# A gated delta-rule layer on one core: four prologues hoisted in front of one stream of 64 heads, sixteen heads written out in the loop's body

## The chip, the core and the metric

The kernel runs on one core of one Trainium2 chip. The metric is device time in microseconds (us). The engines are TensorE (PE, with its weight loads PEld), VectorE (DVE), ScalarE (ACT), GpSimd (POOL) and SyncE (SP), whose queue issues every DMA of this kernel.

## What is computed

Eight sequences of 512 tokens and 256 channels pass through a gated delta-rule attention layer (16 key heads, each with a group of 2 value heads of 128 channels) and a feed-forward block with ternary weights. Cut to what matters here:

```
qkvz = layernorm(x) @ W_qkvz          # per key head: q, k, v, z
qkv  = silu(causal_conv1d(qkv))       # 4 taps
g, beta = decay and gate from layernorm(x) @ W_ba
per chunk of 64 tokens:
    attn = (I + tril(k_beta k^T * decay))^-1
    v'   = attn @ v_beta - k_cumdecay @ state
    out  = q @ state * exp(g) + tril(q k^T * decay) @ v'
    state = state * exp(g_last) + (k * decay)^T @ v'
out = rmsnorm(out * silu(z)) @ W_out  # summed over the heads
```

The feed-forward block works on the same normalized tokens; its result plus `x` is what the heads' outputs are added to (`acc`).

## The kernel before, in words

The batch is cut into four groups of two sequences (`NQ` = 4, `TOK` = 1024 tokens). The four groups are the turns of an outer loop, which every engine runs for itself. A turn has these stages:

- **Prologue.** `x` is loaded into `acc`, normalized and transposed into `xnT` (the transposed tokens that all projections read), the decays and gates are computed, and the feed-forward block is added into `acc`. SP reloads the prepared feed-forward weights and the scan mask (L417 to L419) in each turn, and at the end writes the rows and columns that the heads read (`g_rows`, `ge_rows`, `gel_d`, `cols_d`) to memory and waits for them.
- **Heads.** A head has two halves. Its *front* (`front_piece`, 24 places) projects q, k, v, z, convolves, builds the decay matrix `at` and inverts its triangular part; `at` goes out to memory and comes back in another layout (`relayout`, whose first DMA is `a_d<-at`, L383, one in each head). Its *core* runs over the 8 chunks in order, and its output is projected and added to `acc` up to three chunks later.
- `weave` runs the core of one head with the front of the next head threaded through it, three places of the front at each chunk. `head_passes` (L276) puts a turn together: the front of head 0 by itself, a weave, a loop of 7 iterations with two weaves written out in its body, the core of head 15 by itself, and `last_tile` for the chunks still owed.
- **Store.** When the last `accumulate` is done, SP writes `acc` to `out`, waits until it has landed, and the next turn begins.

The engines meet twice in a turn (`meet`, L270: each drains, adds to a semaphore and waits for all five), before the prologue and behind it. Between the meetings the order of work is that of the code on each engine, held together by counting semaphores, whose targets are worked out in registers from the head's number `g` (L239, L243, L247). `load_weights` (L338) fetches the projection weights `wt` of a head once the last projection of the head before is done, `load_rest` its decay rows `gb`, `qge`, `gel` and its output weights `wo`.

Of the kernel before, what the change touches and what calls it, by code (L numbers as in the profile page):

```python
# [13 lines left out]
P = 128  # L14
# [41 lines left out]
def build(nc, x_in, w_qkvz, w_ba, conv_w, a_log, dt_bias, norm_w, w_out, w_gu, w_proj, consts, out):  # L56
    ctx = ExitStack()
    with ctx:
# [10 lines left out]
        g_rows = dram("g_rows", [HK, NB, NC, GRP, CH])  # L69
        ge_rows = dram("ge_rows", [HV, NC, NB, CH])  # L70
        gel_d = dram("gel_d", [HV, NB, NC])
        cols_d = dram("cols_d", [HK, P, COLS * U])
        a_d = dram("a_d", [P, U, CH])
        x_d = dram("x_d", [P, 2, BLK, BLK])
        wgu_d = dram("wgu_d", [P, KD * 2 * FFN], BF16)
        wp_d = dram("wp_d", [P, FFN // P * D])
# [15 lines left out]
        acc = sb("acc", [P, TILES, D])  # L92
        wt = sb("wt", [P, KD, HEADCOLS])
# [100 lines left out]
        d_const, d_wraw, d_wsave = sem("d_const"), sem("d_wraw"), sem("d_wsave")  # L194
# [123 lines left out]
        def _(sp):  # L318
# [32 lines left out]
            def load_rest(g, p, hk):  # L351
# [5 lines left out]
                             cols_d[bass.ds(hk, 1), :, :].rearrange("a p x -> p (a x)")).then_inc(d_g, 16)  # L357
                for b in range(NB):
                    row = g_rows[bass.ds(hk, 1), b, :, :, :].rearrange("k c h t -> k (c h t)")
# [4 lines left out]
                row = ge_rows.rearrange("(k h) c b t -> k (h c b t)", h=GRP)[bass.ds(hk, 1), :]  # L364
# [5 lines left out]
                             gel_d.rearrange("(k h) b c -> k (h b c)", h=GRP)[bass.ds(hk, 1), :].to_broadcast(  # L370
# [4 lines left out]
                    :, bass.ds(hk * GRP, GRP), :]).then_inc(d_wo, 16)  # L375

# [34 lines left out]

            with sp.Fori(0, NQ) as q:
                meet(sp, 2 * q + 1)
# [11 lines left out]
                for b in range(NB):  # L425
                    rows = slice(b * HV, (b + 1) * HV)
                    for h in range(GRP):
                        sp.dma_start(g_rows[:, b, :, h, :], g_t[b * HV + h:(b + 1) * HV:GRP, :].rearrange(
                            "k (c t) -> k c t", t=CH)).then_inc(d_rows, 16)
                    sp.dma_start(ge_rows[:, :, b, :], ge_t[rows, :].rearrange("p (c t) -> p c t", t=CH)).then_inc(d_rows, 16)  # L430
                    sp.dma_start(gel_d[:, b, :], gelc[rows, :]).then_inc(d_rows, 16)
                sp.wait_ge(colev, (q + 1) * (2 * COLS))
                apart(sp)
                sp.dma_start(cols_d.rearrange("k p x -> p k x"),
                             colstage.rearrange("p k s u -> p k (s u)")).then_inc(d_rows, 16)
                sp.wait_ge(d_rows, (q + 1) * (16 * (NB * (GRP + 2) + 1)))
# [3 lines left out]
                sp.wait_ge(d_wq, (q + 1) * 48)  # L440
                apart(sp)
                meet(sp, 2 * q + 2)

                load_rest(q * HK, 0, 0)
                relayout(q * HK)
                relayout_back(q * HK)
                with sp.Fori(0, HK // 2 - 1) as j:
                    for n in range(2):
                        g, hk = q * HK + j * 2 + (n + 1), j * 2 + (n + 1)
                        load_weights(g, hk)  # L450
                        load_rest(g, (n + 1) % 2, hk)
                        relayout(g)
                        relayout_back(g)
                load_weights(q * HK + (HK - 1), HK - 1)
                load_rest(q * HK + (HK - 1), 1, HK - 1)
                relayout(q * HK + (HK - 1))
                relayout_back(q * HK + (HK - 1))

                before(sp, "accs", q * HK + HK)
                apart(sp)  # L460
                for b in range(NB):
                    sp.dma_start(out.rearrange("b s d -> (b s) d")[bass.ds(q * TOK + b * SEQ, SEQ), :].rearrange(
                        "(c t) d -> t c d", t=CH), acc[half(b), :, :]).then_inc(d_out, 16)
                sp.wait_ge(d_out, (q + 1) * (16 * NB))
                apart(sp)


        @block.tensor
        def _(pe):
# [16 lines left out]
            def prologue(q):  # L486
# [18 lines left out]
                pe.wait_ge(d_wq, (q + 1) * 48)  # L505
# [222 lines left out]
            def front_piece(g, p, s):  # L728
# [7 lines left out]
                for n, at_s in enumerate((1, 2, 4, 5, 5, 8, 10, 13, 13, 14, 14, 16, 17, 20, 22, 22, 23, 23)):  # L736
                    if s == at_s:
                        fill_ring(g, p, n)
# [24 lines left out]
            def front(g, p):  # L763
                for s in range(3 * NC):
                    front_piece(g, p, s)

            def core(g, p, fill=lambda s: None, first=False):
# [3 lines left out]
            def last_tile(g, p):  # L771
# [5 lines left out]
            def weave(g, p, first=False):  # L777
                core(g, p, lambda s: front_piece(g + 1, 1 - p, s), first)

            with pe.Fori(0, NQ) as q:  # L780
                meet(pe, 2 * q + 1)
                prologue(q)
                meet(pe, 2 * q + 2)
                head_passes(pe, q, front, core, weave, last_tile)
# [3 lines left out]
        def _(act):  # L788
# [148 lines left out]
            def front_piece(g, p, s):  # L937
# [21 lines left out]
            def core(g, p, fill=lambda s: None, first=False):  # L959
# [13 lines left out]
            def last_tile(g, p):  # L973
# [5 lines left out]
            def front(g, p):  # L979
                for s in range(3 * NC):  # L980
                    front_piece(g, p, s)

            def weave(g, p, first=False):
                core(g, p, lambda s: front_piece(g + 1, 1 - p, s), first)

            with act.Fori(0, NQ) as q:
                meet(act, 2 * q + 1)
                prologue(q)
                meet(act, 2 * q + 2)
                head_passes(act, q, front, core, weave, last_tile)  # L990
# [3 lines left out]
        def _(dve):  # L994
# [41 lines left out]
            def prologue(q):  # L1036
# [41 lines left out]
                def decay_step(n):  # L1078
# [16 lines left out]
                    if n == 4:  # L1095

                        dve.wait_ge(d_wq, (q + 1) * 48)
# [71 lines left out]
            def decayed_squares(g, p, x):  # L1169
                if x == 0:  # L1170
                    before(dve, "yp", g)
                    loaded(dve, d_off, g - 1, NB * (NBLK - 1))
# [104 lines left out]
            def front_piece(g, p, s):  # L1277
# [28 lines left out]
            def core(g, p, fill=lambda s: None, first=False):  # L1306
                for c in range(NC):
# [5 lines left out]
                    if three:  # L1313
                        accumulate(*three)
# [7 lines left out]
            def last_tile(g, p):  # L1322
                mean_square(g, p, NC - 1)
                for j in (NC - 3, NC - 2, NC - 1):
                    accumulate(g, p, j)

            def front(g, p):
                for s in range(3 * NC):
                    front_piece(g, p, s)

            def weave(g, p, first=False):
                core(g, p, lambda s: front_piece(g + 1, 1 - p, s), first)

            with dve.Fori(0, NQ) as q:
                meet(dve, 2 * q + 1)
                prologue(q)
                meet(dve, 2 * q + 2)
                head_passes(dve, q, front, core, weave, last_tile)
# [3 lines left out]
        def _(pool):  # L1342
# [33 lines left out]
            def front_piece(g, p, s):  # L1376
# [5 lines left out]
            def core(g, p, fill=lambda s: None, first=False):  # L1382
# [10 lines left out]
            def last_tile(g, p):  # L1393
                rms(g, p, NC - 1)

            def front(g, p):
                for s in range(3 * NC):
                    front_piece(g, p, s)

            def weave(g, p, first=False):  # L1400
                core(g, p, lambda s: front_piece(g + 1, 1 - p, s), first)

            with pool.Fori(0, NQ) as q:
                meet(pool, 2 * q + 1)
                prologue(q)
                meet(pool, 2 * q + 2)
                head_passes(pool, q, front, core, weave, last_tile)
# [18 lines left out]
```

## Time and profile before

| | |
|---|---|
| runs shown | 5644.02, 5653.62, 5666.7 us (median 5653.62) |
| profiled execution, its own time | 5670.83 us |
| its span, first to last instruction | 5668.7 us |
| mean granted TensorE clock | 0.948 |
| PE busy | 4973.4 us, 88% of the span |
| DVE, ACT, POOL busy | 62%, 54%, 19% |
| one turn (from one load of `x` to the next) | 1397.6, 1392.5 and 1394.6 us |

The profiled execution's own time is 2.1 us over its span and 0.3% over the median of the runs. The shares are of the span; PE counts as busy while a matmul runs, and its weight loads are a column of their own.

### The profile page before, as it was taken

The numbers are of one execution on the slowest core, as the hardware profiler recorded it, in microseconds if no ns is written. First come the engines' busy times: TensorE is split into PE (matmuls) and PEld (weight loads), VectorE is DVE, ScalarE is ACT, GpSimd is POOL, SyncE is SP. The second block draws the span as 40 slices with busy tenths as digits, with TensorE's granted clock in tenths as the row PEclk, the third lists the DMA queues.
The fourth block names the chain that finished last, engine by engine and source line by source line (L and its number), as shares of the span: only waits on it lengthen the run. The fifth ranks groups of instructions, "written<-read, shape, count | busy, mean of one in ns | idle before, by whom it ended". The sixth has DMA issues, their size and how long they took to land.

```text
span 5668.7 us, 144560 instructions
## 1 busy us (share of the span) xinstructions
PE 4973.4 (88%) x52244; PEld 3458.8 (61%) x52272; DVE 3513.1 (62%) x6423; ACT 3046.6 (54%) x7910; POOL 1063.6 (19%) x1064
## 2 busy tenths in 40 slices
PE   3899999999779999999977999999997899999898
PEld 1566666666556666666645666666664566666666
DVE  6466666666446666666645666666664666666665
ACT  2355555555346555555524655555552555555555
POOL 0022221222111212221211221222220122221122
PEclk7899999999989999999988999999998999999999
DMA  2121222222122221222112222212211221222221
GB/s 68 48 57 42 58 56 53 59 48 53 39 53 54 58 59 43 56 57 54 42 38 59 56 58 53 59 42 58 57 34 44 70 56 46 56 57 54 53 49 38
DMA packets 685930, 296.71 MB, mean 52 GB/s; under 512 B 598976, under 2 KB 642112, under 8 KB 675648
## 3 DMA queue, kind: packets, MB, share of 16 engines
q1 hardware_dynamic: 685120, 286.09, 21.0%
q8 instruction: 486, 7.96, 0.6%
q14 instruction: 324, 2.65, 0.1%
HBM read 213.55 MB, written 59.78 MB: 48 GB/s over the span
## 4 chain that ended last, share of the span: by engine, by line
PE 62%; DVE 11%; ACT 9%; issue 8%; SPq 5%; DMA 3%; DVEq 0%; POOL 0%; ACTq 0%; POOLq 0%
PE pj L587 10%; PE dsb L724 8%; PE ms L645 7%; SPq L409 5%; PE pj L582 4%; ACT arena L856 4%; PE pot L682 4%; PE pot L653 4%; DVE cy L1135 4%; PE dsb L696 3%; PE pod L665 3%; PE ms L600 3%; PE pod L708 2%; PE ms L614 2%; PE pj L577 2%
## 5 line engine op out<-in xcount | busy, mean ns | idle before, releaser
L587 PE MATMUL pj<-xnT,wt 128*128 128x512 f32 x2048 | 1037.2, 636 | 101.0 <-ACT arena L856 58.7
L1135 DVE SCALAR_TENSOR_TENSOR cy<-xpad,cw,cy 128x1024 f32<-128x1024 f32 x768 | 1059.7, 1386 | 33.3 <-ACT cy L876 23.7
L1374 POOL TENSOR_TENSOR rout<-rin,expo 128x2 f32<-128x2 f32 x512 | 366.8, 716 | 2738.7 <-DVE rin L1270 2738.7
L724 PE MATMUL dsb<-wo,yT 128*128 128x256 f32 x2048 | 609.6, 423 | 98.5 <-issue 94.3
L587 PEld LDWEIGHTS pj<-xnT,wt 128*128 128x128 f32 x2048 | 369.1, 198 | 528.4 <-issue 372.7
L1368 POOL TENSOR_TENSOR sdec<-st,gel 128x512 f32<-128x512 f32 x384 | 402.2, 1047 | 1047.5 <-DVE st L1259 866.2
L875 ACT ACTIVATE xpad<-pj 128x512 f32<-128x512 f32 x512 | 302.5, 591 | 500.5 <-PE pj L587 499.7
L934 ACT ACTIVATE yT<-dsb 128x256 f32<-128x256 f32 x512 | 196.2, 383 | 644.6 <-PE dsb L715 643.2
L582 PE MATMUL pj<-wt,xnT 128*128 128x256 f32 x2048 | 511.7, 393 | 0.0
L724 PEld LDWEIGHTS dsb<-wo,yT 128*128 128x128 f32 x2048 | 365.9, 199 | 217.7 <-issue 180.5
L1249 DVE SCALAR_TENSOR_TENSOR rr<-pot,nge,arena 128x128 f32<-128x128 f32 x896 | 271.2, 344 | 338.6 <-PE pot L653 338.6
L582 PEld LDWEIGHTS pj<-wt,xnT 128*128 128x128 f32 x2048 | 371.4, 191 | 86.5 <-issue 43.9
L1259 DVE TENSOR_TENSOR st<-dsb,sdec 128x512 f32<-128x512 f32 x384 | 264.8, 690 | 220.9 <-PE dsb L696 216.5
L929 ACT ACTIVATE arena<-arena,rout 128x128 f32<-128x128 f32 x1024 | 351.6, 393 | 43.4 <-POOL rout L1374 43.0
L923 ACT ACTIVATE junk<-arena 128x128 f32<-128x128 f32 x1024 | 306.4, 307 | 96.0 <-issue 53.7
L1270 DVE SCALAR_TENSOR_TENSOR rin<-ss,qe 128x2 f32<-128x2 f32 x512 | 80.1, 156 | 437.4 <-ACT junk L923 437.4
L876 ACT ACTIVATE cy<-pj,cw 128x512 f32<-128x512 f32 x512 | 348.4, 680 | 0.0
L696 PEld LDWEIGHTS dsb<-ww,arena 64*128 64x128 f32 x3584 | 238.4, 186 | 175.1 <-issue 167.0
L1275 DVE TENSOR_TENSOR acc<-dsb,acc 128x256 f32<-128x256 f32 x512 | 215.9, 422 | 201.0 <-PE dsb L724 192.9
L682 PE MATMUL pot<-rr,bda 64*64 64x128 f32 x3584 | 293.2, 281 | 53.7 <-DVE rr L1249 53.7
L696 PE MATMUL dsb<-ww,arena 64*128 64x128 f32 x3584 | 325.0, 297 | 16.5 <-ACT ww L917 16.4
L708 PE MATMUL pod<-ww,arena 64*64 64x128 f32 x4096 | 332.2, 281 | 2.3 <-ACT ww L917 2.3
(163 smaller groups left out, 8502.6 us busy)
## 6 DMA issues: line engine op xcount, KB each, us to landing
qge<-ge_rows SPq DMA_DIRECT2D x64, 1024.0 KB, 7.0
wt<-in_L_attn_W_qkvz SPq DMA_DIRECT2D x64, 768.0 KB, 4.4
gb<-g_rows SPq DMA_DIRECT2D x128, 256.0 KB, 4.1
a_d<-at SPq DMA_DIRECT2D x64, 512.0 KB, 2.6
wo<-in_L_attn_W_out SPq DMA_DIRECT2D x64, 256.0 KB, 2.7
x_d<-xpair SPq DMA_DIRECT2D x128, 128.0 KB, 1.7
ap_<-a_d SPq DMA_DIRECT2D x512, 16.0 KB, 1.8
dd<-x_d SPq DMA_DIRECT2D x512, 16.0 KB, 1.8
```

The source lines that it names most:

```text
L582: last = mm(pj[n % 2][:, v * GRP * DH:(v + 1) * GRP * DH], xnT[:, k, c * P:(c + 1) * P], wt[:, k, 4 * DH:4 * DH + GRP * DH], start=(k == 0 ...
L587: last = mm(pj[n % 2][:, :], wt[:, k, col:col + DH], batch(xnT, k, i), start=(k == 0), stop=(k == KD - 1))
L645: last = mm(ms[n][half(b), v * CH:(v + 1) * CH], pbd[half(b), u, :], src[half(b), u, :], start=True, stop=True, tile_position=(b * CH, b * ...
L682: last = mm(pkw[half(b), (GRP + h) * DH:(GRP + h + 1) * DH], bda[half(b), p, c * GRP + h, :], rhs, start=True, stop=True, tile_position=(b ...
L696: last = mm(dsb[:, b, h * DH:(h + 1) * DH], kkd[p][half(b), c * GRP + h, :], ww[half(b), h, :], start=True, stop=True, tile_position=(b * ...
L708: last = mm(po[half(b), h * DH:(h + 1) * DH], it[half(b), p, c * GRP + h, :], ww[half(b), h, :], start=(c == 0), stop=True, skip_group_che ...
L724: last = mm(dsb[:, 0, GRP * DH:GRP * DH + D], yT[:, h, :], wo[:, p, h, :], start=(h == 0), stop=(h == GRP - 1))
L876: last = fn(cy[:, m % 2, i, :], src[:, :], ACT.Copy, scale=cw[:, m, TAPS - 1:TAPS])
L929: last = fn(zz[p][:, j, h, :], zz[p][:, j, h, :], ACT.Copy, scale=rout[:, h:h + 1])
L1135: stt(y, x[:, :, tap:tap + SEQ], cw[:, kind, tap:tap + 1], y, ALU.mult, ALU.add).then_inc(S["conv"], 1)
L1368: tt(sdec[:, :, :, :], st[:, c % 2, :, :, :], bc(gel[:, p, :, :].rearrange("p h (b c) -> p b h c", b=NB)[:, :, :, c], 3, DH), ALU.mult).th ...
L1374: tt(rout[:, :], rin[:, :], expo[:, 0, 0:GRP], ALU.pow).then_inc(S["routs"], 1)
```

## The change

All engines now run the four prologues in one loop, and then the 64 heads as one stream (`head_stream`): the front of head 0, a weave, a loop of 3 iterations with sixteen weaves written out, 14 more weaves written out behind it, and the core of the last head. What a prologue leaves for its heads goes to memory with a place for each group: the rows and columns as before, and in addition `xnT_d` (1 MB, the transposed tokens) and `base_d` (1 MB, `x` plus the feed-forward block). When the stream comes to the first head of a group, SP loads that group's `xnT` behind `wt`, and `base` behind `wo`; the first head's `accumulate` reads `base` instead of `acc`. The output is stored in two parts while the next group's first heads run (chunks 0 to 4, then 5 to 7). The feed-forward weights stay on chip through the four prologues, so their saving and reloading is gone, and the scan mask is loaded once. In the body of the loop the head's number within its group is a constant, and in the stretches outside the loop all wait targets are.

```diff
-        def head_passes(eng, q, front, core, weave, last_tile):
-            front(q * HK, 0)
-            weave(q * HK, 0, True)
-            with eng.Fori(0, HK // 2 - 1) as j:
-                weave(q * HK + j * 2 + 1, 1)
-                weave(q * HK + j * 2 + 2, 0)
-            core(q * HK + (HK - 1), 1)
-            last_tile(q * HK + (HK - 1), 1)
+        def head_stream(eng, front, core, weave, last_tile):
+            front(0, 0)
+            weave(0, 0, True)
+            with eng.Fori(0, NQ - 1) as q:
+                for n in range(1, HK + 1):
+                    weave(q * HK + n, n % HK)
+            for n in range((NQ - 1) * HK + 1, NQ * HK - 1):
+                weave(n, n % HK)
+            core(NQ * HK - 1, HK - 1)
+            last_tile(NQ * HK - 1, HK - 1)
...
             sp.wait_ge(q_ev, 12)
-            sp.dma_start(wgu_d, wguT.rearrange("p k n -> p (k n)")).then_inc(d_wsave, 16)
-            sp.dma_start(wp_d, wpT.rearrange("p i n -> p (i n)")).then_inc(d_wsave, 16)
-            sp.wait_ge(d_wsave, 32)
+            sp.dma_start(scanmask, consts[:, SCANMASK:CONSTS]).then_inc(d_wq, 16)
+            sp.wait_ge(d_wq, 16)
...
+            def load_tokens(g, q):
+                sp.dma_start(xnT[:, :, :].rearrange("p k t -> p (k t)"), xnT_d[bass.ds(q, 1), :, :].rearrange(
+                    "q p x -> p (q x)")).then_inc(d_xn, 16)
...
+                if hk == 0:
+                    sp.dma_start(base[:, :, :].rearrange("p t d -> p (t d)"), base_d[bass.ds(q, 1), :, :].rearrange(
+                        "q p x -> p (q x)")).then_inc(d_base, 16)
...
+            def head(g, q, hk, weights=True, stores=True):
+                if weights:
+                    load_weights(g, hk)
+                if hk == 0:
+                    load_tokens(g, q)
+                load_rest(g, q, hk)
+                if hk == 1 and stores:
+                    store(q - 1, NC - 3, NC)
+                relayout(g)
+                relayout_back(g)
+                if hk == 0 and stores:
+                    after(sp, "accs", g - 1, NC - 3)
+                    apart(sp)
+                    store(q - 1, 0, NC - 3)
+
+            load_weights(0, 0)
+            meet(sp, 1)
             with sp.Fori(0, NQ) as q:
-                meet(sp, 2 * q + 1)
...
-                sp.dma_start(wguT.rearrange("p k n -> p (k n)"), wgu_d).then_inc(d_wq, 16)
-                sp.dma_start(wpT.rearrange("p i n -> p (i n)"), wp_d).then_inc(d_wq, 16)
-                sp.dma_start(scanmask, consts[:, SCANMASK:CONSTS]).then_inc(d_wq, 16)
-                load_weights(q * HK, 0)
+                sp.wait_ge(xntev, (q + 1) * (TILES // 2))
+                apart(sp)
+                sp.dma_start(xnT_d[bass.ds(q, 1), :, :].rearrange("q p x -> p (q x)"),
+                             xnT[:, :, :].rearrange("p k t -> p (k t)")).then_inc(d_rows, 16)
...
+                sp.wait_ge(facc, (q + 1) * TILES)
+                apart(sp)
+                sp.dma_start(base_d[bass.ds(q, 1), :, :].rearrange("q p x -> p (q x)"),
+                             acc[:, :, :].rearrange("p t d -> p (t d)")).then_inc(d_rows, 16)
...
-                meet(sp, 2 * q + 2)
...
+                meet(sp, q + 2)
+
+            head(0, 0, 0, weights=False, stores=False)
+            head(1, 0, 1, stores=False)
+            with sp.Fori(0, NQ - 1) as q:
+                for n in range(2, HK + 2):
+                    head(q * HK + n, q + n // HK, n % HK)
+            for n in range((NQ - 1) * HK + 2, NQ * HK):
+                head(n, NQ - 1, n % HK)
...
-            def fill_ring(g, p, n):
+            def fill_ring(g, p, n, new_tokens):
                 kind, i = ring[n]
                 if n == 0:
                     loaded(pe, d_w, g, 4)
+                    if new_tokens:
+                        pe.wait_ge(d_xn, g + HK)
...
-            def accumulate(g, p, j):
+            def accumulate(g, hk, j):
+                if hk == 0 and j == 0:
+                    dve.wait_ge(d_base, g + HK)
+                if hk == 0 and j in (0, NC - 3) and not (type(g) is int and g == 0):
+                    dve.wait_ge(d_out, g * 4 + (0 if j else -32))
                 after(dve, "od", g, j + 1)
-                tt(acc[:, j, :], dsb[:, 0, GRP * DH:GRP * DH + D], acc[:, j, :], ALU.add).then_inc(S["accs"], 1)
+                tt(acc[:, j, :], dsb[:, 0, GRP * DH:GRP * DH + D], (acc if hk else base)[:, j, :], ALU.add
+                   ).then_inc(S["accs"], 1)
```

On PE, in the program before, this is what stands at the end of the loop's body: the last chunk of the second weave, and the branch back to its first (`L577` is the last turned `v`, `L280` the loop).

```order
L645 MATMUL ms<-at,pbd 64x64 x16
L239 REGISTER_ALU
L708 MATMUL pod<-ww,arena 64x128 x4
L239 REGISTER_ALU
L577 MATMUL pj<-cst,vT 128x128 x4
L239 REGISTER_ALU
L577 MATMUL pj<-cst,vT 128x128 x4
L280 REGISTER_ALU
L280 COMPARE_AND_BRANCH
```

In the changed program the same last chunk, at the end of the second weave of the written-out body, runs into the first projection of the output in the third weave (`L754` is what was L724, `L607` what was L577).

```order
L675 MATMUL ms<-at,pbd 64x64 x16
L241 REGISTER_ALU
L738 MATMUL pod<-ww,arena 64x128 x4
L241 REGISTER_ALU
L607 MATMUL pj<-cst,vT 128x128 x4
L241 REGISTER_ALU
L607 MATMUL pj<-cst,vT 128x128 x4
L754 MATMUL dsb<-wo,yT 128x256 x2
L745 MATMUL dsb<-cst,arena 128x128 x2
L241 REGISTER_ALU x2
```

The register step and the branch are gone from this place; they stand once, behind the sixteenth weave. Behind the loop, in the weaves whose numbers are constants, PE's code has no register rows at all; this is its start:

```order
L283 COMPARE_AND_BRANCH
L754 MATMUL dsb<-wo,yT 128x256 x2
L745 MATMUL dsb<-cst,arena 128x128 x2
L712 MATMUL pot<-arena,bda 64x128 x4
L617 MATMUL pj<-xnT,wt 128x512 x2
L726 MATMUL dsb<-ww,arena 128x128 x4
```

On SP's queue, in the program before, a group ends with the return of the last head's inverse, the store of `out`, and the branch of the outer loop.

```order
L409 DMA ee<-x_d 16x16x16 x8
L243 ISA
L462 DMA out<-acc 64x8x256 x2
L412 REGISTER_ALU
L412 COMPARE_AND_BRANCH
```

In the changed program the queue goes from a group's first head (its inverse returns, `L427`) over the first part of the store (`L361`) to the weights of the second head (`L347`).

```order
L427 DMA ee<-x_d 16x16x16 x8
L241 REGISTER_ALU
L361 ISA
L361 DMA out<-acc 64x5x256
L361 ISA
L361 DMA out<-acc 64x5x256
L241 REGISTER_ALU
L245 ISA
L347 DMA wt<-in_L_attn_W_qkvz 128x2x768
```

The store, with its wait for five accumulations of the head before, now stands ahead of a load of weights, where it stood alone.

## Rows read from the trace of the kernel before

**Rows 1.** The page: span; PE's busy time and instructions; a queue that carries instructions.

```profile
span 5668.7 us, 144560 instructions
PE 4973.4 (88%) x52244; PEld 3458.8 (61%) x52272; DVE 3513.1 (62%) x6423; ACT 3046.6 (54%) x7910; POOL 1063.6 (19%) x1064
...
q8 instruction: 486, 7.96, 0.6%
```

**Rows 2.** Busy time by stage: prologue, weaves, core alone; then clock, DMA share, GB/s.

```profile
94.00:207.00 113.00, 87.88 (x441) 56.18 (x448) 54.53 (x103) 31.90 (x54) 8.30 (x9) 0.88 0.15 45
...
365.00:1420.00 1055.00, 967.25 (x10640) 676.77 (x10639) 688.12 (x1270) 611.59 (x1626) 218.92 (x218) 0.97 0.23 54
1420.00:1487.00 67.00, 51.00 (x604) 38.52 (x600) 28.08 (x66) 26.89 (x95) 13.32 (x17) 0.97 0.08 18
```

**Rows 3.** SP's queue in order of time: start, duration, line; setup and first two turns.

```profile
86.91 0.35 SPq L334 DMA_DIRECT2D wgu_d<-arena  x1
...
93.82 1.60 SPq L415 DMA_DIRECT2D acc<-in_L_attn_x  x2
...
207.41 0.36 SPq L356 DMA_DIRECT2D cols<-cols_d  x1
...
231.65 0.33 SPq L383 DMA_DIRECT2D a_d<-at  x1
...
1491.41 1.56 SPq L415 DMA_DIRECT2D acc<-in_L_attn_x  x2
...
1603.07 0.36 SPq L356 DMA_DIRECT2D cols<-cols_d  x1
...
1626.12 0.33 SPq L383 DMA_DIRECT2D a_d<-at  x1
```

**Rows 4.** SP's queue: `a_d<-at` of heads 1, 3, 4, 5, 15 of group 0.

```profile
297.48 0.33 SPq L383 DMA_DIRECT2D a_d<-at  x1
...
447.78 0.33 SPq L383 DMA_DIRECT2D a_d<-at  x1
...
528.23 0.33 SPq L383 DMA_DIRECT2D a_d<-at  x1
...
602.39 0.33 SPq L383 DMA_DIRECT2D a_d<-at  x1
...
1387.37 0.33 SPq L383 DMA_DIRECT2D a_d<-at  x1
```

**Rows 5.** The same, last head of a group and first of the next, twice.

```profile
2780.03 0.33 SPq L383 DMA_DIRECT2D a_d<-at  x1
...
3020.25 0.32 SPq L383 DMA_DIRECT2D a_d<-at  x1
...
4173.00 0.34 SPq L383 DMA_DIRECT2D a_d<-at  x1
...
4415.01 0.32 SPq L383 DMA_DIRECT2D a_d<-at  x1
```

**Rows 6.** Waits: who, what ended them, us in total, times, longest.

```profile
PE dsb L724 <- issue: 94.3, 24, 4.9
...
POOL gb L1356 <- DMA gb<-g_rows: 255.9, 8, 45.8
```

**Rows 7.** The chain that ended last: start, us, what; a loop's branch, then the outer loop's.

```profile
495.27 3.95 issue
...
1488.23 2.72 issue
```

**Rows 8.** Busy time by engine right behind that first branch, granted clock third from the end.

```profile
499.30:503.00 3.70, 3.70 (x15) 2.55 (x16) 1.24 (x3) 0.84 (x4) 2.57 (x2) 0.54 0.02 7
```

**Rows 9.** DMA issues: count, KB each, median us from issue to landing.

```profile
arena<-wgu_d SPq DMA_DIRECT2D x4, 1024.0 KB, 8.5
...
cols_d<-arena SPq DMA_DIRECT2D x4, 512.0 KB, 3.9
```

**Rows 10.** Register steps of L247 on the weight loads' sequencer: ns shortest/median/longest.

```profile
L247 PEldq FUSED_REGOPS  x192: 37/37/51, 207.0 to 5596.3; - x192
```

More of the change, by code:

```diff
@@ L66, in dram @@
             return nc.dram_tensor(name, shape, dt, kind="Internal").ap()
[L69 to L72, printed above, removed]
+        g_rows = dram("g_rows", [NQ, HK, NB, NC, GRP, CH])
+        ge_rows = dram("ge_rows", [NQ, HV, NC, NB, CH])
+        gel_d = dram("gel_d", [NQ, HV, NB, NC])
+        cols_d = dram("cols_d", [NQ, HK, P, COLS * U])
+        xnT_d = dram("xnT_d", [NQ, P, KD * TOK])
+        base_d = dram("base_d", [NQ, P, TILES * D])
         a_d = dram("a_d", [P, U, CH])
         x_d = dram("x_d", [P, 2, BLK, BLK])
-        wgu_d = dram("wgu_d", [P, KD * 2 * FFN], BF16)
-        wp_d = dram("wp_d", [P, FFN // P * D])
         cst = sb("cst", [P, SCANMASK])
@@ L92, in build @@
         acc = sb("acc", [P, TILES, D])
+        base = sb("base", [P, TILES, D])
         wt = sb("wt", [P, KD, HEADCOLS])
@@ L349, in load_weights, with store, load_rest @@
                     "(h p) t -> p h t", h=GRP)).then_inc(d_w, 16)
-            def load_rest(g, p, hk):
+            def load_tokens(g, q):
+                sp.dma_start(xnT[:, :, :].rearrange("p k t -> p (k t)"), xnT_d[bass.ds(q, 1), :, :].rearrange(
+                    "q p x -> p (q x)")).then_inc(d_xn, 16)
+            def store(q, j0, j1):
+                for b in range(NB):
+                    sp.dma_start(out.rearrange("b s d -> (b s) d")[
+                        bass.ds(q * TOK + (b * SEQ + j0 * CH), (j1 - j0) * CH), :].rearrange("(c t) d -> t c d", t=CH),
+                        acc[half(b), j0:j1, :]).then_inc(d_out, 16)
+            def load_rest(g, q, hk):
+                p = hk % 2
                 before(sp, "coef", g)
@@ L439, in _ @@
                 apart(sp)
-                sp.wait_ge(d_wq, (q + 1) * 48)
-                apart(sp)
-                meet(sp, 2 * q + 2)
[L444 to L465, printed above, removed]
+                meet(sp, q + 2)
[6 more added lines that the diff above has]
+                head(n, NQ - 1, n % HK)
+            for j0, j1 in ((0, NC - 3), (NC - 3, NC)):
+                after(sp, "accs", NQ * HK - 1, j1)
+                apart(sp)
+                store(NQ - 1, j0, j1)
+            sp.wait_ge(d_out, NQ * (4 * 16))
         @block.tensor
@@ L761, in core_step, with front, core, last_tile @@
                 fill(3 * c + 2)
-            def front(g, p):
+            def front(g, hk):
                 for s in range(3 * NC):
-                    front_piece(g, p, s)
-            def core(g, p, fill=lambda s: None, first=False):
+                    front_piece(g, hk, s)
+            def core(g, hk, fill=lambda s: None, first=False):
+                p = hk % 2
                 for c in range(NC):
                     core_step(g, p, c, fill, first)
-            def last_tile(g, p):
+            def last_tile(g, hk):
+                p = hk % 2
                 out_project(g, p, NC - 3)
@@ L775, in last_tile, with weave @@
                     out_project(g, p, j)
-            def weave(g, p, first=False):
-                core(g, p, lambda s: front_piece(g + 1, 1 - p, s), first)
+            def weave(g, hk, first=False):
+                core(g, hk, lambda s: front_piece(g + 1, (hk + 1) % HK, s), first)
+            meet(pe, 1)
             with pe.Fori(0, NQ) as q:
-                meet(pe, 2 * q + 1)
                 prologue(q)
-                meet(pe, 2 * q + 2)
-                head_passes(pe, q, front, core, weave, last_tile)
+                meet(pe, q + 2)
+            head_stream(pe, front, core, weave, last_tile)
         @block.scalar
@@ L957, in front_piece, with core @@
                             squares(g, p, 0)
-            def core(g, p, fill=lambda s: None, first=False):
+            def core(g, hk, fill=lambda s: None, first=False):
+                p = hk % 2
                 for c in range(NC):
@@ L977, in last_tile, with front, weave @@
                 output_columns(g, p, NC - 1)
-            def front(g, p):
+            def front(g, hk):
                 for s in range(3 * NC):
-                    front_piece(g, p, s)
-            def weave(g, p, first=False):
-                core(g, p, lambda s: front_piece(g + 1, 1 - p, s), first)
+                    front_piece(g, hk, s)
+            def weave(g, hk, first=False):
+                core(g, hk, lambda s: front_piece(g + 1, (hk + 1) % HK, s), first)
+            meet(act, 1)
             with act.Fori(0, NQ) as q:
-                meet(act, 2 * q + 1)
                 prologue(q)
-                meet(act, 2 * q + 2)
-                head_passes(act, q, front, core, weave, last_tile)
+                meet(act, q + 2)
+            head_stream(act, front, core, weave, last_tile)
         @block.vector
@@ L1171, in decayed_squares @@
                     before(dve, "yp", g)
-                    loaded(dve, d_off, g - 1, NB * (NBLK - 1))
+                    if not (type(g) is int and g == 0):
+                        loaded(dve, d_off, g - 1, NB * (NBLK - 1))
                 else:
@@ L1304, in front_piece, with core @@
                         decayed_queries(g, p, h)
-            def core(g, p, fill=lambda s: None, first=False):
+            def core(g, hk, fill=lambda s: None, first=False):
+                p = hk % 2
                 for c in range(NC):
@@ L1313, in core @@
                     if three:
-                        accumulate(*three)
+                        accumulate(three[0], hk if c >= 3 else (hk - 1) % HK, three[2])
                     fill(3 * c)
@@ L1320, in core, with last_tile, front, weave @@
                     fill(3 * c + 2)
-            def last_tile(g, p):
+            def last_tile(g, hk):
+                p = hk % 2
                 mean_square(g, p, NC - 1)
                 for j in (NC - 3, NC - 2, NC - 1):
-                    accumulate(g, p, j)
-            def front(g, p):
+                    accumulate(g, hk, j)
+            def front(g, hk):
                 for s in range(3 * NC):
-                    front_piece(g, p, s)
-            def weave(g, p, first=False):
-                core(g, p, lambda s: front_piece(g + 1, 1 - p, s), first)
+                    front_piece(g, hk, s)
+            def weave(g, hk, first=False):
+                core(g, hk, lambda s: front_piece(g + 1, (hk + 1) % HK, s), first)
+            meet(dve, 1)
             with dve.Fori(0, NQ) as q:
-                meet(dve, 2 * q + 1)
                 prologue(q)
-                meet(dve, 2 * q + 2)
-                head_passes(dve, q, front, core, weave, last_tile)
+                meet(dve, q + 2)
+            head_stream(dve, front, core, weave, last_tile)
         @block.gpsimd
@@ L1380, in front_piece, with core @@
                     key_norms(g)
-            def core(g, p, fill=lambda s: None, first=False):
+            def core(g, hk, fill=lambda s: None, first=False):
+                p = hk % 2
                 for c in range(NC):
```

65 lines of the change are left out of this document (38 added, 27 removed).

## The prediction

> **What bounds the kernel now.** I read the page first: PE is busy for 88% of the span and everything else far less [rows 1]. Then the busy time by stage, since an average hides stages. In the weaves PE works 967 of 1055 us at a granted clock of 0.97; in a prologue 88 of 113 us; where a core runs alone 51 of 67 us [rows 2]. So in a weave the bound is PE's own work and short waits around it, and what can be had without less work lies elsewhere: in the stretches where front and core do not cover each other, and in PE's idle time inside the loop. For these I read SP's queue in order of time, because it issues `a_d<-at` once in each head, always behind the same step of the front: the distance between two of them is a head's period.
>
> Inside an iteration of the loop that period is 528.23 to 602.39 = 74.2 us; across the branch back it is 447.78 to 528.23 = 80.5 us [rows 4]. The same reading over the whole trace gives 74.9 us in the mean of 28 distances inside an iteration (73.7 to 77.9) and 81.5 us in the mean of 24 across a branch (79.3 to 84.8). The ends agree: from head 1 to head 15 of group 0 are 1089.9 us, against 14 x 74.9 + 6 x 6.6 = 1088.2 [rows 4]. The waits show the cause on PE: before the first matmul of a weave, L724, it idled 94.3 us in 24 times, released by nothing that the profile shows; 24 is the number of branches (6 in each of 4 groups), so 3.9 us each [rows 6]. The chain passes through that very gap at 495.27 for 3.95 us [rows 7], and in the 3.7 us behind it the granted clock is 0.54, mostly the lower level of 1.2 GHz, where the weaves have 0.97 [rows 8, 2]. Idle time, slower matmuls and the other engines' later restart make up the 6.6 us.
>
> **The change, part by part.** All sums are made against the profiled execution's span of 5668.7 us [rows 1].
>
> *Branches inside the heads.* 24 become 2 (3 iterations of sixteen weaves): 22 x (81.5 - 74.9) = **-145.2 us**. The order rows show that nothing else moves there: the same matmuls, without a branch between them.
>
> A page of the Trainium skill speaks against this term: "Advanced Engine Details and Errata", section Control Flow Timing, gives about 108 ns for a compare-and-branch. As an estimate by that figure, the term would be 22 x 0.1 = 2 us and the whole sum some 143 us smaller. The 3.9 us of [rows 6] decide. "Runtime: NRT & Kernel Launch", section Instruction fetch mechanics, says that a taken branch out of the code at hand has to fetch its target first, and that purely sequential code is prefetched; by that rule the term stands, and the trace's gap agrees.
>
> *Seams.* From the last `a_d<-at` of a group to the first of the next are 238.75, 240.2 and 242.0 us, mean 240.3 [rows 3 to 5]. Of it the prologue, from loading `x` to loading `cols`, is 111.7 us in group 1 and 113.6 in group 0, mean 112.6 [rows 3]. It is only moved. The other 127.7 us (rest of the last weave, a core alone, last tile, store, meeting, a front alone up to `at`) become one distance of the stream, 74.9: 3 x 52.8 = **-158.4 us**. On the other side, the first distance of a group, whose core owes no output of an earlier head, was 231.65 to 297.48 = 65.8 us [rows 3, 4] and becomes 74.9 in three groups: **+27.3 us**.
>
> *Prologues.* Reloading the weights cost no path time that I can see, since DVE waits only for `x`. Its traffic behind `x` is gone; I give that 0.5 us in each, -2.0. New on SP's path at the end are `base_d`, issued behind the rows, and its landing together with `cols_d`. The nearest rows: 512 KB of `cols_d` land in 3.9 us and 1 MB of weights in 8.5 us [rows 9], so 1 MB more costs between nothing and 8.5; as the two overlap I take 2.5, and 0.4 for the issue: 4 x 2.9 = +11.6. The `xnT_d` store goes out while SP would wait. The branch of the prologue loop stands between a meeting and the load of `x`: SP's outer branch cost 2.7 us before [rows 7] and hit the seam, so three of these are already in the seam's gain; three may come back, or none if SP's short code is still at hand; I take half, +4.2. The other engines' branches hide under the load of `x`. Together **+13.8 us**.
>
> *Head 0 of the stream* must wait for its tokens to come back before its first projection: nothing to 8.5 us [rows 9]; as nothing covers it, near the upper end, **+6.5**.
>
> *First heads of groups 1 to 3.* The 1 MB of tokens stands ahead of `gb` and `qge`; `base` has a whole weave to land. At the second head SP waits for `accumulate` of chunk 4 before it issues the store and only then `wt`; behind it queue `cw`, `cols`, `gb`, and PE's first projection and POOL's L1356 wait for them. Cost between nothing and 8.5 us for the tokens, and about the same for the store. POOL waited for `gb` in 8 of 64 heads [rows 6], so there is slack; I take 4 us a seam, **+12**.
>
> *Setup and end.* From 86.91 to 93.82 the weights are saved [rows 3]; now 256 KB are loaded, and `wt` is issued ahead of the meeting. The last store is smaller. **-2.7**.
>
> *Constants.* Outside the loop, 14 weaves, a front and a core have no register rows. One register step takes 37 ns [rows 10] and PE's code has about 31 in a weave, 1.1 us; mostly they run while the engine waits anyway. Between nothing and 1.1 us for 15 heads (17 us); I take 0.4 each, **-6**.
>
> The stream's weave itself I leave at 74.9 us.
>
> Sum: -145.2 - 158.4 + 27.3 + 13.8 + 6.5 + 12 - 2.7 - 6 = -252.7 us. Span 5416.0, own time 2.1 more, 5418.1. The profiled execution took 5670.83 us against a median of 5653.62; in the same ratio the median becomes **5402 us**, 4.5% less.
>
> **The rivals.** *A, half of the branches' excess stays.* If the engines only catch up later what the pause let them get ahead of (SP and the DMAs run on through it), the straight stream runs at a longer period: 22 x 3.3 = 73 us come back, 5475 us. For it: the 3.9 us of PE's idle time are only part of the 6.6. Against it: head 1 to head 3, with no branch between and none ahead, took 150.3 us, 75.2 each [rows 4]. Chance 0.13.
>
> *B, the stream runs faster.* Behind each branch PE's clock was low [rows 8], and register steps go; if a head needs 74.0 us, 62 x 0.9 = 56 us more, 5346. Chance 0.08.
>
> *C, slower than before: the supply of code.* Sixteen written-out weaves are eight times the loop's body. If the old body was kept on chip and the new one must be fetched, PE pauses all along. The queue for instructions carried 486 packets, 7.96 MB, at 0.6% of 16 engines' span, that is 0.006 x 16 x 5668.7 / 486 = 1.1 us each; 7.6 in a head [rows 1]. If each stood open, 7.6 x 1.1 x 62 = 518 us: 5920 us. It decides from 252.7 / 62 = 4.1 us a head, half of each fetch. Against it: 7.96 MB over the 104,516 matmuls and weight loads are 76 bytes each, so the loop's body was fetched anew in every iteration already, and PE's pauses without a releaser are those 24 at the branches and no others of any size. Chance 0.03.
>
> *D, no change.* The seam's overlap fails: first heads that wait for tokens, `base` and the store in turn for some 80 us a seam. The loads are 1 MB each, 8.5 us at most [rows 9], so it would take a wait that I have not seen. With smaller failures of that sort, chance 0.03.
>
> **How the numbers follow.** My forecast has 0.73: 5402, in its own range of about 5365 to 5440 (0.5 us in the period of 62 heads are 31 us; the seams' loads may be 0 or 50 us; three prologue branches 0 or 8). The range takes in B and A: 5345 to 5480. A difference of 0.5%, 28 us, is about what a measurement of this kernel can tell from no change. Faster: forecast, A and B, 0.94; C gives most of slower, 0.04; the same 0.02.
>
> **What would show it.** The wait of PE before the output projection L754 with no releaser: 2 times, about 8 us in all. `a_d<-at` at even distances of 75 us through the loop, near 81 at two places only, and 75 to 83 at a group's first and second head. Four prologues at 114 to 118 us each, the first `a_d<-at` near 590 us. One stretch with PE busy 51 of 67 us, at the end. Instruction packets fewer by the branches' refetches and not more. The prediction is wrong if the distances in the stream are 76 us or more, if PE shows waits without a releaser inside the weaves, if heads 16, 32 and 48 stand out by more than 15 us, or if a prologue takes over 125 us.

## The result, and the profile after

| | median, us | range, runs | ratio to the kernel before (95%) |
|---|---|---|---|
| before | 5655.99 | 5644.02 to 5666.7, 4 | |
| changed | 5450.92 | 5436.97 to 5453.92, 4 | 0.9633 (0.9607 to 0.9659) |
| changed, measured again beside the variants | 5446.68 | 5441.0 to 5457.37, 5 | 0.9610 (0.9587 to 0.9632) |

The changed kernel is 3.7 to 3.9% faster; forecast were 5402 us (4.5%) in a range of 5345 to 5480. The page of its profiled execution (5436.97 us) answers to [rows 1]:

```profile
span 5434.8 us, 140777 instructions
PE 4886.2 (90%) x52272; PEld 3409.1 (63%) x52272; DVE 3511.8 (65%) x6423; ACT 3036.7 (56%) x7909; POOL 1063.5 (20%) x1064
...
q8 instruction: 428, 7.01, 0.5%
```

The same matmuls are done in a span that is 234 us shorter, and PE's busy time falls by 87 us of it; the mean granted clock went from 0.948 to 0.963. The queue q8, which carries instructions, has 58 packets fewer.

SP's queue in order of time (start, duration, line) answers to [rows 3 to 5]: the first two loads of `x`, the first `cols` and `a_d<-at` of head 0, then `a_d<-at` of heads 15 to 18, with the weights, tokens and store between them (cut by "...").

```profile
91.67 1.58 SPq L449 DMA_DIRECT2D acc<-in_L_attn_x  x2
...
208.23 1.60 SPq L449 DMA_DIRECT2D acc<-in_L_attn_x  x2
...
555.09 0.33 SPq L371 DMA_DIRECT2D cols<-cols_d  x1
...
580.05 0.33 SPq L401 DMA_DIRECT2D a_d<-at  x1
...
1702.91 0.33 SPq L401 DMA_DIRECT2D a_d<-at  x1
...
1740.03 0.40 SPq L347 DMA_DIRECT2D wt<-in_L_attn_W_qkvz  x1
...
1742.09 0.34 SPq L356 DMA_DIRECT2D xnT<-xnT_d  x1
...
1777.25 0.33 SPq L401 DMA_DIRECT2D a_d<-at  x1
...
1819.21 1.57 SPq L361 DMA_DIRECT2D out<-acc  x2
1821.14 0.63 SPq L347 DMA_DIRECT2D wt<-in_L_attn_W_qkvz  x1
...
1855.07 0.34 SPq L401 DMA_DIRECT2D a_d<-at  x1
...
1941.02 0.33 SPq L401 DMA_DIRECT2D a_d<-at  x1
```

From a group's last head to the next group's first are 1777.25 - 1702.91 = 74.3 us, where 240.3 stood. From first to second head are 77.8 us (80.7 and 80.3 at the other two), and here the weights are issued 43.9 us behind the head's `a_d`, behind the store, and not 37.1 us as one head earlier. The next distance, 86.0 us, holds the loop's branch; at the second branch it is 85.2, and in the last group, where no branch stands, 75.7. The other distances inside the loop are 75.3 us in the mean of 43, those of the last group 74.7 in the mean of 14.

PE's waits (us in total, times, longest) answer to [rows 6]:

```profile
PE pj L617 <- DMA xnT<-xnT_d: 14.7, 1, 14.7
PE dsb L754 <- issue: 12.5, 2, 6.7
PE pj L617 <- DMA cw<-in_L_attn_conv_weight: 9.5, 3, 3.6
```

The wait with no releaser stands 2 times instead of 24, but is 6.3 us long instead of 3.9. New are three waits for the convolution's weights `cw`, which are loaded with `wt`, one in each seam, and one for the tokens, at head 0. The chain (start, us, what) and the busy time right behind the gap answer to [rows 7, 8]; the granted clock there is 0.50, the lower level.

```profile
1905.83 5.77 issue
```
```profile
1911.60:1915.30 3.70, 3.70 (x15) 2.57 (x16) 1.48 (x2) 0.41 (x2) 2.56 (x2) 0.50 0.04 9
```

### The profile page after: what moved, and what is told of

It is laid out like the page before. It is cut to its first block, busy times and chain, and to the rows that moved or that the text cites. A ratio compares the mean times of both kernels' runs of the same rounds, so it can differ in the third digit from the quotient of the medians.

```text
span 5434.8 us, 140777 instructions
## 1 busy us (share of the span) xinstructions
PE 4886.2 (90%) x52272; PEld 3409.1 (63%) x52272; DVE 3511.8 (65%) x6423; ACT 3036.7 (56%) x7909; POOL 1063.5 (20%) x1064
## 4 chain that ended last, share of the span: by engine, by line
PE 56%; issue 15%; DVE 10%; ACT 8%; SPq 5%; DMA 3%; POOL 2%; DVEq 0%; POOLq 0%; ACTq 0%
PE pj L617 9%; PE dsb L754 7%; PE ms L675 6%; SPq L427 4%; PE pj L612 4%; ACT arena L889 4%; PE pot L683 4%; PE pot L712 3%; DVE cy L1171 3%; PE pod L695 3%; PE dsb L726 3%; PE ms L644 2%; PE ms L630 2%; PE pod L738 2%; PE ms L659 2%
## 5 line engine op out<-in xcount | busy, mean ns | idle before, releaser
L617 PE MATMUL pj<-xnT,wt 128*128 128x512 f32 x2048 | 1005.5, 619 | 86.6 <-ACT arena L889 56.6
L617 PEld LDWEIGHTS pj<-xnT,wt 128*128 128x128 f32 x2048 | 354.6, 190 | 490.4 <-issue 347.2
L754 PE MATMUL dsb<-wo,yT 128*128 128x256 f32 x2048 | 588.3, 411 | 13.7 <-issue 12.5
L754 PEld LDWEIGHTS dsb<-wo,yT 128*128 128x128 f32 x2048 | 357.0, 194 | 126.2 <-issue 95.8
L726 PEld LDWEIGHTS dsb<-ww,arena 64*128 64x128 f32 x3584 | 235.8, 187 | 164.2 <-issue 155.6
L683 PE MATMUL pot<-st,kq 128*64 128x256 f32 x1792 | 314.7, 427 | 4.7 <-DVE st L1298 2.6
```

The costliest lines, as they stand in the source:

```text
L617: last = mm(pj[n % 2][:, :], wt[:, k, col:col + DH], batch(xnT, k, i), start=(k == 0), stop=(k == KD - 1))
L683: last = mm(pkw[half(b), 0:GRP * DH], kq[:, p, c, b, :], st[:, c % 2, b, :, :].rearrange("p h d -> p (h d)"), start=True, stop=True, tile_ ...
L726: last = mm(dsb[:, b, h * DH:(h + 1) * DH], kkd[p][half(b), c * GRP + h, :], ww[half(b), h, :], start=True, stop=True, tile_position=(b * ...
L754: last = mm(dsb[:, 0, GRP * DH:GRP * DH + D], yT[:, h, :], wo[:, p, h, :], start=(h == 0), stop=(h == GRP - 1))
```

## The experiments

All ratios are to the kernel before on the same chip, whose median there was 5664 to 5673 us. A distance is the time from one head's `a_d<-at` to the next, and each is read from one profiled execution.

**1. The branches alone.** The kernel before with its inner loop written out in each of the four turns.

```diff
-            with eng.Fori(0, HK // 2 - 1) as j:
+            for j in range(HK // 2 - 1):
                 weave(q * HK + j * 2 + 1, 1)
                 weave(q * HK + j * 2 + 2, 0)
...
-                with sp.Fori(0, HK // 2 - 1) as j:
+                for j in range(HK // 2 - 1):
```

> The kernel before with only the inner loop gone: the 14 weaves of each turn are written out on all engines, the outer loop with its prologue, core alone and store stays. 24 branches go. My theory, 6.6 us for each branch: 5656 - 158 = about 5498 us, distances between the heads' a_d stores inside a turn near 75 us everywhere, and PE's wait before L724 without a releaser gone. Rival A, half of that comes back: 5577 us, distances near 78. Rival C, supply of code: not faster than before.

Measured: 5532.09 us, ratio 0.9757 (0.9738 to 0.9775), 138 us less; 139.0 by the spans (5668.7 to 5529.7). That is 5.8 us for each of 24 branches, not 6.6. SP's queue, heads 1 and 15 of the first turn:

```profile
292.16 0.32 SPq L383 DMA_DIRECT2D a_d<-at  x1
...
1351.42 0.32 SPq L383 DMA_DIRECT2D a_d<-at  x1
```

14 distances in 1059.3 us are 75.7 each, and over all four turns, from head 2 on, the mean is 75.5, where the old distances inside an iteration had 74.9. PE's wait before L724 with no releaser is gone. So the branches' price is real, and an eighth of their apparent excess was not: the distances beside a branch had been the shorter for it. Rival C falls here.

Of the 139 us, 127 lie between head 1 and head 15 of the four turns, where the branches stood; that is 5.3 us for each. Another 9 lie in the four distances from head 0 to head 1 (64.0 us in the mean instead of 66.1) and 3 ahead of the first `a_d<-at`. Nothing here shows why, so 5.8 us is the upper reading of a branch's price and 5.3 the lower.

**2. The seams alone.** The changed kernel with short loops put back into the stream (on SP in the same way, heads 3 to 14 of each group; with that, the rows of a head are addressed by its number in all 64).

```diff
             with eng.Fori(0, NQ - 1) as q:
-                for n in range(1, HK + 1):
-                    weave(q * HK + n, n % HK)
-            for n in range((NQ - 1) * HK + 1, NQ * HK - 1):
-                weave(n, n % HK)
+                weave(q * HK + 1, 1)
+                weave(q * HK + 2, 2)
+                with eng.Fori(0, HK // 2 - 2) as j:
+                    weave(q * HK + j * 2 + 3, 3)
+                    weave(q * HK + j * 2 + 4, 4)
+                weave(q * HK + (HK - 1), HK - 1)
+                weave(q * HK + HK, 0)
+            last = (NQ - 1) * HK
+            weave(last + 1, 1)
+            weave(last + 2, 2)
+            with eng.Fori(0, HK // 2 - 2) as j:
+                weave(j * 2 + (last + 3), 3)
+                weave(j * 2 + (last + 4), 4)
```

> The changed kernel with the branches put back: hoisted prologues and one stream, but the weaves of heads 3 to 14 of each group run in a loop of 6 iterations with two weaves in its body. 20 more branches than the changed kernel, and the last group loses its constant wait targets. My theory: 5451 + 20 x 6.6 + 15 x 0.5 = about 5590 us, which would make the seams with all their costs worth 66 us and the rest of the gain the branches'. Rival A: 5451 + 66 + 8 = 5525 us.

Measured: 5590.3 us, ratio 0.9857 (0.9836 to 0.9878). PE's waits show all 22 branches again, 4.7 us each:

```profile
PE dsb L772 <- issue: 104.1, 22, 6.1
```

With the branches left in, the four prologues in front save 1.4%, 81 us. Two branches fewer are some 12 of them, which leaves 69 us for the seams, if a branch costs what it did before. But PE idled longer at these 22 branches (104.1 us) than at the old 24 (94.3 us, [rows 6]), so the seams are worth some 10 us more than these 69.

**3. Everything written out.** The changed kernel without its loop: 62 weaves in a row, all wait targets constants (on SP in the same way).

```diff
-            with eng.Fori(0, NQ - 1) as q:
-                for n in range(1, HK + 1):
-                    weave(q * HK + n, n % HK)
-            for n in range((NQ - 1) * HK + 1, NQ * HK - 1):
+            for n in range(1, NQ * HK - 1):
                 weave(n, n % HK)
```

> The changed kernel with the stream's loop written out altogether: 62 weaves without a branch, all wait targets constants. The two branches cost 10.7 us each in the changed kernel's trace (86.0 and 85.2 against 75.3), and the weaves with constant targets took 74.7 us against 75.3: 5451 - 21 - 48 x 0.56 = about 5403 us. If the constants do nothing and the last group was only luckier: 5430 us. If a longer stretch of code that is never repeated is fed worse (rival C): slower than 5451.

Measured: 5411.85 us, ratio 0.9544 (0.9528 to 0.9560), 37 us under the changed kernel's 0.9610. The distances away from the seams are 74.9 us in the mean. But from a group's first to its second head they are 81.5, 81.5 and 81.2 us, and PE waits there for `cw`:

```profile
PE pj L611 <- DMA cw<-in_L_attn_conv_weight: 12.5, 3, 4.4
```

**4. The store behind the weights**, at the second head of a group, in the changed kernel.

```diff
                 if weights:
                     load_weights(g, hk)
+                if hk == 1 and stores:
+                    after(sp, "accs", g - 2, NC - 3)
+                    apart(sp)
+                    store(q - 1, 0, NC - 3)
...
-                if hk == 0 and stores:
-                    after(sp, "accs", g - 1, NC - 3)
-                    apart(sp)
-                    store(q - 1, 0, NC - 3)
```

> The changed kernel with the first part of the store moved behind the load of the second head's weights on SP's queue (it was ahead of it, with its wait for accumulate). If the order on the queue is what made the distance from first to second head 4.3 us longer (79.6 against 75.3), three seams give 13 us: about 5438 us, and these distances near 75. If the 1 MB loads or the store's traffic are the cause: 5451 us, distances as before.

Measured: 5444.42 us, ratio 0.9601 (0.9585 to 0.9617); against 0.9633 and 0.9610 that settles nothing. The distances from first to second head fell to 76.6, 74.9 and 77.3, and PE no longer waits for `cw`. But the distances ahead of them are 77.7, 79.8 and 75.5 us, and from head 15 to head 18 the three seams together are only 3 us shorter than in the changed kernel.

**5. Both together**: experiments 3 and 4 in one kernel.

> All 62 weaves written out, as in the third experiment, and the first part of the store behind the second head's weights, as in the fourth. In the third the distance from a group's first to its second head was 81.4 us in the mean against 74.9 elsewhere, with no branch near. If SP's order is the cause, it falls to about 77 and three seams give 3 x 4.5 = 13 us: ratio to before about 0.952 against 0.9544 without the move. If the delay only moves to the next head: distances after it longer, and the ratio as without the move.

Measured: 5395.62 us, ratio 0.9512 (0.9490 to 0.9534), the fastest of all, 4.9% under the kernel before; experiment 3's interval just touches it. The profiled execution was the slowest of its five: its span, 5406.3 us, is 3.5 us longer than experiment 3's. SP's queue in the first seam, heads 15, 16 and 17, with the weights now ahead of the store:

```profile
1701.93 0.33 SPq L398 DMA_DIRECT2D a_d<-at  x1
...
1780.86 0.33 SPq L398 DMA_DIRECT2D a_d<-at  x1
...
1820.11 0.40 SPq L344 DMA_DIRECT2D wt<-in_L_attn_W_qkvz  x1
...
1824.59 1.37 SPq L358 DMA_DIRECT2D out<-acc  x2
...
1857.59 0.33 SPq L398 DMA_DIRECT2D a_d<-at  x1
```

The second head's distance is 76.7 us (76.5 and 77.8 at the others) instead of 81.5. The order on the queue was the cause of the long second distance. Yet the distance ahead of it is now 78.9 us (78.3, 73.5), so that from head 15 to head 18, and at the other seams alike, the trace shows only 0.5, 1.6 and 3.5 us less than in experiment 3. Why the first head's distance grew, with nothing moved ahead of it, stays open. It may in part be spread: the changed kernel, measured again with the store in its old place, has 77.9, 75.3 and 74.8 us there. What the move is worth in the whole is thus not shown: between nothing and the 18 us (0.0032) of the two ratios.

**6. The kernel before, everything written out**: experiment 1 with the outer loop written out as well, on all engines, still four turns (PE's lines shown).

```diff
-            with pe.Fori(0, NQ) as q:
+            for q in range(NQ):
```

> The kernel before with every loop written out, the outer one too: no branch at all, all wait targets constants, but still four turns of prologue, heads and store. Against the first experiment (5532 us on this scale) the constants give 56 x 0.45 = 25 us and the three outer branches about 8: 5499 us. The difference to the third experiment (all written out, one stream) is then what the seams alone are worth, with all costs of the tokens and of base: about 87 us. If the constants do nothing: 5524 us.

Measured: 5487.66 us, ratio 0.9680 (0.9654 to 0.9706). Against experiment 1 that is 44 us for constants and three outer branches, where 25 and 8 were expected. SP's queue, last head of the first group and first of the second:

```profile
1340.09 0.32 SPq L383 DMA_DIRECT2D a_d<-at  x1
...
1576.82 0.32 SPq L383 DMA_DIRECT2D a_d<-at  x1
```

236.7 us (234.1 and 235.8 at the others), mean 235.5, where the loop had 240.3: 14 us of the 44 in three seams. The other 30 are 0.5 us in each of 60 heads. Against experiment 3 (0.9544) the seams alone are worth 0.0136, 77 us.

**7 to 9. Where the loop's code lies.** The changed kernel with 64, 128 or 192 waits that are long fulfilled, on PE, between the prologues and the stream.

```diff
+            for _ in range(64):
+                pe.wait_ge(d_const, 16 * 7)
             head_stream(pe, front, core, weave, last_tile)
```

> The changed kernel with 64 waits on a semaphore that has long been reached, on PE alone, once, between the prologues and the stream: all that changes behind them is at what address PE's loop begins. PE's two gaps at the branch were 5.8 and 6.7 us, with two instruction packets of 16 KB in each, where the short loop's had 3.6 to 4.9 us and one. If where the target lies in a block of code decides whether one or two blocks must come, one of the three shifts gives gaps near 4 us with one packet. If the length of the body decides, all three stay at 5.5 to 6.7.

> The same with 128 waits; expectation as for 64: by the place of the target, gaps near 4 us with one packet at one of the shifts; by the length of the body, 5.5 to 6.7 us at all.

> The same with 192 waits; by the place of the target, gaps near 4 us with one packet at one of the three shifts; by the length of the body, 5.5 to 6.7 us at this one too.

One run each: 5451.94, 5458.09, 5457.16 us, no gain to be seen in the whole. But PE's gaps at the two branches shrank at all three shifts, 6.8, 6.9 and 7.5 us for both together against 12.5 (10.9 when measured again, 11.6 in experiment 4). The wait with 64:

```profile
PE dsb L754 <- issue: 6.8, 2, 3.5
```

The queues inside the first gap (packets, MB, share of 16 engines), first the changed kernel's from 1905.8 to 1911.6 us, then that with 64 waits, from 1909.8 to 1913.2:

```profile
q8 instruction: 2, 0.03, 4.5%
q14 instruction: 5, 0.04, 2.5%
```
```profile
q14 instruction: 3, 0.02, 2.1%
q8 instruction: 1, 0.02, 1.7%
```

With one packet on q8 the gap is 3.3 us, with two 5.8; the other gaps of these kernels show the same numbers of packets. The length of the loop's body is not what made it dearer; the place of its code is. [Rows 6] and the changed kernel's waits alone would have spoken for the length. Experiment 2 bears this out: its short loop stands in the code twice, with two weaves in the body each time. The copy that serves the first three groups has one packet in each of its 15 gaps (3.4 to 5.6 us), the copy of the last group has two in each of its 5 (5.1 to 5.3 us).

Why the whole did not gain the 5 us is not shown. The distances across the branches fell (80.4 to 83.5 us, against 82.4 to 86.0 in the changed kernel's two traces), but the other distances in the loop are 75.6, 75.6 and 75.7 us instead of 75.3 and 75.4, and with 192 waits the first `a_d<-at` comes 5 us later.

## Why the prediction was right, and what was mis-sized

Both sources of the gain, the branches and the seams, were right, and none of the signs of being wrong came: the stream's distances are 75.3 us, heads 16, 32 and 48 stand at 74.0 to 75.7, and no prologue takes over 117 us. The sizes were less good, and in part they made up for each other. The forecast span was 5416.0 us, the measured one 5434.8. By its steps:

- **Branches, -145.2.** Right in kind: experiment 1 takes them away and nothing else. Mis-sized twice. One costs 5.8 us, not 6.6: rival A in a small part. And the two that are left cost 86.0 - 75.3 and 85.2 - 75.3, some 10.3 us each, for which I had 6.6 (in the trace measured again 82.4 and 85.8, 8.8 us each). So the term is 24 x 5.8 - 2 x 10.3 = 119 us, in which the next point is already contained.
- **The stream's weave, left at 74.9.** This is the step that failed. I took the distances inside an iteration as what straight code would show, though each stood beside a branch. Straight code with register targets has 75.3 (the loop here) and 75.5 (experiment 1). 0.4 us in 48 heads are 19 us, and it is the other face of the first point. The prediction had 75.2 us each from head 1 to head 3 [rows 4], and used it only against rival A.
- **Seams.** My seam terms (-158.4, +27.3, prologues +13.8, tokens +6.5, first heads +12, setup and end -2.7) make -101.5. Of them 14 us were the outer branches and the constants of these stretches, as experiment 6 shows, which leaves 87; the difference of experiments 3 and 6 is 77, experiment 2's reading 69 or more. Experiment 3's second heads cost 6.5 us each where I had 4: that is 7 of the 10.
- **First heads, +12.** The tokens cost nothing (74.3, 74.0 and 75.7 us at heads 15 to 16); SP's order cost 77.8, 80.7, 80.3 less 75.3, together 13. The trace shows the wait I had described, for `cw`. That the two terms of this estimate gave the right sum was luck: one was nothing, the other all of it.
- **Prologues, +13.8.** They took 116.6, 115.0, 116.6 and 115.3 us, together 13 us over 4 x 112.6. `cols_d`, with `base_d` beside it, lands in 5.9 us instead of 3.9 [rows 9].
- **Head 0, +6.5.** From `cols` to `a_d<-at` are 580.05 - 555.09 = 25.0 us, against 24.2 and 23.1 in [rows 3]: about 1 us. PE waited 14.7 us for the tokens and started its first projection at 559.6, but POOL started on the decay rows `gb` only at 562.7, and the chain up to `a_d<-at` goes through `gb`.
- **Constants, -6.** 74.7 against 75.3 in the last group's 14 distances, 8 us; experiments 1 and 6 give 0.5 a head. The bound from register steps held.
- **Setup and end, -2.7.** `x` is loaded at 91.67 instead of 93.82; from the last `a_d<-at` to the end are 94.4 us where 100.2 were, a gain that I had not listed and did not take apart.

Added up by the landmarks of the trace: from head 1 to head 15 of the four groups are 4351.4 us before and 4231.3 after, 120 less, where branches and constants were to give 151. Of the 31 us that are missing some 8 are the two dearer branches and most of the rest the longer weave. The seams and second heads came out 2 us over the sum, and the stretches ahead of the first `a_d<-at` and behind the last 13 us under it (580.1 and 94.5 us, where the sum has 587.1 and 100.2). That is 20 us, and 19 were measured; without the savings at the two ends, of which I had foreseen less than 3 us, the span would have been off by some 32. The other 30 of 5451 - 5402 come from carrying a ratio of profiled executions over to medians: the spans' ratio is 0.9587, the timed ones 0.9633 and 0.9610, since the profiled execution before lay above its median and the one after was the fastest of its four. The prediction's own range for its forecast, about 5365 to 5440, did not hold the 5451 and 5447 us; the wider one did, by the room that rival A had given it.

Rival D (seams that fail) did not come; B (74.0 us a head) neither, even in experiment 3. Rival C was refuted by experiments 1 and 3: the longest stretch of straight code is the fastest, and q8 carried 486 packets before, 428 after, 416 with everything written out, so fewer branches meant less code fetched. The Trainium skill's figure for a compare-and-branch ("Advanced Engine Details and Errata", Control Flow Timing, about 108 ns) would have put the branches' term near 2 us. The runs show 138. The Trainium skill ("Runtime: NRT & Kernel Launch", Instruction fetch mechanics) says that a taken branch out of the code at hand has to fetch its target before it goes on; the one or two instruction packets inside each gap agree.

## What to carry to other kernels

Look for waits with no releaser at the head of a loop's body and count them against its iterations; if PE is the bound, writing the body out can be worth more than the restructuring that it comes with (here 138 us for 24 branches against 77 for the seams). When such a stop is priced from the distances between landmarks, the stretches beside it are no clean base: compare total with total, or take the stop away. And when a store with a wait is woven into a stream, look at what is queued behind it: here the next head's weights came 7 us later and PE waited for them, though moving the store gained less in the whole than at that place.

## What the runs showed of the hardware that I had not expected

What a branch of PE's loop cost in idle time went with the number of instruction packets of q8 in its gap. In the kernel before it was 3.6 to 4.9 us, with one packet, at all 24 branches. In the changed kernel it was 5.4 to 6.7 us, with two (two traces, and experiment 4's), and 3.3 to 3.8 us, with one, once the same code lay 64 or more instructions further on. It is no full rule: one gap of experiment 2 is 5.6 us long with one packet, another 5.1 with two.

SP's own branch is as uneven: 2.7 us at the old outer loop [rows 7], and at the new prologue loop under 0.3 us from the branch to SP's next register step. Constant wait targets were worth some 0.5 us in each head on a stream that PE bounds.
